# A vision block rewritten per tile of four images: own semaphores and PSUM banks, weights laid out on the host

## The reference

```python
x = x + _L0_conv_ref(_ln_c(x), L0_conv_W_trans)       # q, k, v; softmax over the 3x3 neighbours, 4 heads
t = _to_tokens(x)
t = t + _L0_ffn_ref(_ln_t(t), ...)                    # expert choice: 16 experts take their top 8 tokens of 576
x = _from_tokens(t, x)
x = x + _L1_conv_ref(_ln_c(x), ...)                   # 9x9 patches: y = a @ (b.T @ c) / 9 over 81 patch entries
t = _to_tokens(x)
t = t + _L1_ffn_ref(_ln_t(t), ...)                    # scan of 33 steps; the op is the argmax of token 0
x = _from_tokens(t, x)

def step(h, p):                                       # of _L1_ffn_ref
    op = jnp.argmax(h[0, 0, :NOPS])
    ...                                               # attention, kept only where p['am'][op]
    z = jax.nn.relu(h @ p['w1'][op] + p['b1'][op]) @ p['w2'][op] + p['b2'][op]
    h = jnp.where(p['fm'][op], z, h)
```

## Time and profile before

| what | us |
|---|---|
| median of 3 runs | 162.72 (161.98 to 163.53) |
| span of the profiled execution | 158.8 |
| PE busy | 136.2 (86%) |
| DVE busy | 94.5 (60%) |
| POOL busy | 55.2 (35%) |
| ACT busy | 48.9 (31%) |

### The profile page before, as it was taken

The page is one execution under the profiler, slowest core; times in us unless marked ns, Lnnn a source line. Parts: engine busy times, 40 slices in busy tenths (PEclk is TensorE's granted clock), DMA queues, the critical chain, the costliest instruction groups (busy, mean ns, idle before and its releaser), DMA issues.

```text
span 158.8 us, 2235 instructions
## 1 busy us (share of the span) xinstructions
PE 136.2 (86%) x819; PEld 88.7 (56%) x819; DVE 94.5 (60%) x153; ACT 48.9 (31%) x98; POOL 55.2 (35%) x50
## 2 busy tenths in 40 slices
PE   7959733989999975999899989889999998989960
PEld 4628412655664442666574666663349887567540
DVE  2496699998999999954730122274213122854573
ACT  3460600019000011533734004302262152648540
POOL 8930699000747789999600000000000000027000
PEclk9999995599999999789985555999999999999998
DMA  5525000000000000000000000000000000000003
GB/s 164 136 14 124 15 4 0 0 4 0 2 0 0 0 0 0 0 4 0 0 2 0 0 4 0 0 0 0 0 0 4 0 0 0 0 12 15 0 4 151
DMA packets 7374, 2.62 MB, mean 16 GB/s; under 512 B 5680, under 2 KB 6978, under 8 KB 7363
## 3 DMA queue, kind: packets, MB, share of 16 engines
q1 hardware_dynamic: 7075, 2.04, 5.5%
q10 hardware_dynamic: 288, 0.43, 0.8%
HBM read 1.88 MB, written 0.59 MB: 16 GB/s over the span
## 4 chain that ended last, share of the span: by engine, by line
PE 48%; DVE 40%; ACT 3%; issue 3%; DMA 2%; SPq 1%; DVEq 0%; ACTq 0%
DVE prods L1042 9%; DVE prods L1075 8%; PE PS L709 6%; PE PS L523 6%; PE PS L847 5%; PE PS L493 4%; DVE prods L1093 4%; PE PS L499 4%; PE PS L729 3%; PE PS L742 3%; PE PS L722 3%; DVE rstd L1022 3%; PE PS L700 2%; DMA cst<-consts 2%; PE PS L658 2%
## 5 line engine op out<-in xcount | busy, mean ns | idle before, releaser
L326 POOL TENSOR_TENSOR y<-x,h 128x192 f32<-128x192 f32 x6 | 3.9, 688 | 63.9 <-DVE h L1032 63.9
L493 PE MATMUL PS<-sq 128*128 128x288 f32 x48 | 20.1, 550 | 1.1 <-POOL sq L407 1.1
L876 ACT ACTIVATE sq<-PS 128x288 f32<-128x288 f32 x16 | 6.5, 413 | 41.7 <-PE PS L614 23.7
L1042 DVE TENSOR_TENSOR prods<-q_sb,kpad 128x576 f32<-128x576 f32 x12 | 14.8, 1304 | 2.0 <-ACT kpad L904 2.0
L432 POOL TENSOR_TENSOR prods<-q_sb,kpad 128x576 f32<-128x576 f32 x6 | 10.7, 1822 | 8.2 <-ACT kpad L904 8.2
L577 PE MATMUL PS<-prods,cst 128*32 128x144 f32 x144 | 8.1, 359 | 6.3 <-DVE prods L1042 6.3
L493 PEld LDWEIGHTS PS<-sq 128*128 128x128 f32 x48 | 10.4, 245 | 4.8 <-issue 1.7
L1075 DVE TENSOR_TENSOR prods<-PS,vpad 128x576 f32<-128x576 f32 x18 | 12.5, 745 | 0.0
L523 PE MATMUL PS<-rstd,spread 128*128 128x144 f32 x64 | 8.9, 292 | 3.3 <-DVE rstd L1022 3.3
L523 PEld LDWEIGHTS PS<-rstd,spread 128*128 128x128 f32 x64 | 8.0, 190 | 5.5 <-DVE rstd L1022 5.5
L577 PEld LDWEIGHTS PS<-prods,cst 128*32 128x32 f32 x144 | 4.6, 135 | 9.6 <-DVE prods L1042 8.6
(11 more groups left out here) (165 smaller groups left out, 249.0 us busy)
## 6 DMA issues: line engine op xcount, KB each, us to landing
result<-y SPq DMA_DIRECT2D x2, 288.0 KB, 2.2
prods<-in_x SPq DMA_DIRECT2D x2, 144.0 KB, 3.4
prods<-in_x ACTq DMA_DIRECT2D x1, 288.0 KB, 4.0
ew<-in_L_ffn_weight SPq DMA_DIRECT2D x4, 64.0 KB, 2.5
ew<-in_L_ffn_weight SPq DMA_DIRECT2D x1, 256.0 KB, 3.0
cst<-consts SPq DMA_DIRECT2D x1, 251.0 KB, 3.3
cst<-consts SPq DMA_DIRECT2D x1, 160.0 KB, 3.1
cst<-consts ACTq DMA_DIRECT2D x1, 128.0 KB, 3.4
```

Source lines behind the costliest of these rows:

```text
L493: nc.tensor.matmul(PS[:, bank, 0:HS], sq[:, 0, 0:P], sq[:, 0, 0:HS], start=True, stop=True)
L1042: nc.vector.tensor_tensor(prods[:, t, n, :].rearrange("p (r c) -> p r c", c=WW), q_sb[:, t, :].rearrange("p (r c) -> p r c", c=WW), kpad[: ...
```

## The change

The arithmetic is the same; the kernel around it is written anew.

- **Weights and tables** come laid out from the host in eight arrays (`first`, `pack`, `qkv`, `experts1`, `experts2`, `values`, `masks`, `codes`): block-diagonal weights, selectors, the 65-wide patch matrices. Nothing is turned or built on the chip, and `keep_clock` is gone with all its products.
- **Per tile.** Each tile has its own semaphores and PSUM banks (`AB[t]`, `CD[t]`), and the tiles run shifted: one is in its norm while the other is in its products.
- **Norm.** Ln and Exp with scale -0.5 on ACT give the inverse deviation; the reciprocal on DVE is gone. `widen` uses 64-row selectors.
- **Attention.** q stays in PSUM for DVE's products (POOL reads a copy); v goes by halves through one bank; the softmax's sum is nine products on PE, its inverse Ln and Exp on ACT, and DVE scales the weights before they are spread. `spread` uses four strips of 32 rows, one per quarter of the pixels, each into its own bank; DVE multiplies 24 times (`terms`), POOL adds (`gsum`), PE centres each sum as it comes (`add_centred`).
- **Experts.** `pick` is turned by a product with a diagonal matrix that scales it; hidden has the expert's weights (128 columns) stationary and the four images' tokens moving (16 products a tile); the centring of the next norm is folded into the scatter (`keep_centred`, `scatter`), with a second, uncentred scatter for the residual. ACT changes tables to gelu and back for each tile.
- **conv1.** Groups of 13 channels, laid in runs; one `mab` product of 390 columns with 65 rows per patch row; gram and value of a group come from one product (117 by 181 columns).
- **FFN.** The first layer uses four 32-row strips with one copy of the weights; relu is shared by ACT and DVE; the next op is found from relu and the second weights directly; one operation adds bias and residual. The weights' transfers wait for `step_end`, which DVE gives after the last residual of conv1.

The diff, cut to its core:

```diff
-            def keep_clock(n, bank):
-                for i in range(n):
-                    nc.tensor.matmul(PS[:, bank, 0:HS], sq[:, 0, 0:P], sq[:, 0, 0:HS], start=True, stop=True)
+            def widen(i, t):
+                pe.wait_ge(rstd_rdy[t], i + 1)
+                pe.wait_ge(xc_kept[t], 2 * i + 2)
+                for g in range(2):
+                    for par in range(2):
+                        last = nc.tensor.matmul(PS[:, AB[t][g], par * QS:(par + 1) * QS], sel[64 * g:64 * g + 64, par, :],
+                                                rstd[64 * g:64 * g + 64, t, :], start=True, stop=True)
...
+            def spread(u):
+                t, m = divmod(u, TRI)
+                if t == 0:
+                    pe.wait_ge(attn_rdy, m + 1)
+                for q in range(4):
+                    if u >= 1:
+                        pe.wait_ge(term_rdy, 4 * (u - 1) + q + 1)
+                    nc.tensor.matmul(PS[:, 4 + q, 0:TRI * QS], heads[32 * q:32 * q + 32, t, :],
+                                     attn[32 * q:32 * q + 32, m * TRI:(m + 1) * TRI, :].rearrange("k n s -> k (n s)"),
+                                     start=True, stop=True).then_inc(spread_done, 1)
...
+            def hidden(t):
+                nc.tensor.matmul(PS[:, CD[t][0], 0:ER], con("eb1", E_), con("ebsel", E_), start=True, stop=False, skip_group_check=True)
+                pe.wait_ge(pm_rdy[t], 1)
+                for e in range(E_):
+                    last = nc.tensor.matmul(PS[:, CD[t][0], e * TB:(e + 1) * TB], ew1[:, e, :], pm[:, t, e * TB:(e + 1) * TB],
+                                            start=False, stop=True, skip_group_check=True)
...
+            def expert_out(t):
+                pe.wait_ge(hid_rdy[t], 1)
+                for e in range(E_):
+                    last = nc.tensor.matmul(PS[0:C, CD[t][1], 128 + e * TB:128 + (e + 1) * TB], ew2[:, e, :],
+                                            hidT[:, t, e * TB:(e + 1) * TB], start=False, stop=True, skip_group_check=True)
...
+            def scatter(t):
+                pe.wait_ge(ebd_rdy[t], 1)
+                for g in range(2):
+                    nc.tensor.matmul(PS[:, AB[t][g], 0:HS], flat[:, 1, :], cut(pick, t)[:, g, :], start=False, stop=True,
+                                     skip_group_check=True).then_inc(xc_done[t], 1)
+                pe.wait_ge(ebd_rdy[t], 2)
+                for g in range(2):
+                    nc.tensor.matmul(PS[:, CD[t][g], 0:HS], flat[:, 0, :], cut(pick, t)[:, g, :], start=True,
+                                     stop=True).then_inc(raw_done[t], 1)
...
+            def gsum(t, m):                                     # POOL
+                a = prods[:, t, m * TRI, :]
+                pool.wait_ge(term_rdy, 4 * (TRI * t + m + 1))
+                total = prods[:, 1, 1, :] if (t, m) == (1, 2) else a
+                nc.gpsimd.tensor_tensor(total, a, prods[:, t, m * TRI + 1, :], ALU.add).then_inc(gsum_rdy[t], 1)
+                if m < TRI - 1:
+                    pool.wait_ge(gsum_rdy[t], 2 * m + 1)
+                    nc.gpsimd.tensor_tensor(a, a, prods[:, t, m * TRI + 2, :], ALU.add).then_inc(gsum_rdy[t], 1)
...
+            def product(t, n):                                  # DVE, q in PSUM
+                dy, dx = divmod(n, 3)
+                k = kpad[:, t, dy:dy + HH, dx:dx + WW].rearrange("p (g r) c -> p g r c", g=2)
+                nc.vector.tensor_tensor(prods[:, t, n, :].rearrange("p (g r c) -> p g r c", g=2, c=WW), rows24(both(AB[t])), k,
+                                        ALU.mult).then_inc(prod_rdy[t], 1)
...
+            def inverse_std(i, t):                              # ACT
+                nc.scalar.activation(lnv[:, t, :], PS[:, AB[t][0], 0:QS], ACT.Ln, bias=con(EPS[i])).then_inc(ln_rdy[t], 1)
+                act.wait_ge(ln_rdy[t], i + 1)
+                nc.scalar.activation(rstd[:, t, :], lnv[:, t, :], ACT.Exp, scale=-0.5).then_inc(rstd_rdy[t], 1)
...
+            gram_mask(0, 4)                                     # DVE, conv1
+            residual3(0, 0)
+            choose(0, 0)
+            residual3(0, 1)
+            residual3(0, 2)
+            for k in range(4):
+                gram_mask(1, k)
```

More of the change, by code:

```diff
@@ L24 @@
 V2 = RV * RV
+V2A = V2 + 1
+GRP = 13
+NG = 10
+GW = GRP * NPT
+CP = NG * GRP
 BAND = NP * V2
[L26 to L28 removed]
 NB_, NOPS = 33, 19
[L30 to L41 removed]
@@ new lines, in _ @@
+            pe.wait_ge(gsum_rdy[1], 2)
+            add_centred(1, prods[:, 1, 0, :])
+            widen(1, 0)
+            spread(5)
+            gate(0)
+            pe.wait_ge(gsum_rdy[1], 4)
+            add_centred(1, prods[:, 1, 3, :])
+            for g in range(2):
+                pe.wait_ge(term_rdy, 4 * 5 + 2 * g + 2)
+                for n in (6, 7, 8):
+                    add_centred(1, prods[:, 1, n, :], last=(n == 8), halves=(g,))
+            turn_y(0)
+            variance(1, 1)
@@ new lines, in _ @@
+            turn_pick(0)
+            widen(1, 1)
+            pe.wait_ge(ew1_ld, 16)
+            pe.wait_ge(ew2_ld, 16)
+            pooling(0)
+            keep_centred(0)
+            gate(1)
+            hidden(0)
+            turn_y(1)
+            turn_pick(1)
+            expert_out(0)
+            pooling(1)
+            keep_centred(1)
+            scatter(0)
+            hidden(1)
+            variance(2, 0)
+            expert_out(1)
+            widen(2, 0)
+            scatter(1)
@@ L906, in _, with squares, keep, squares_keep @@
-            for i in range(4):
-                qkv_out(i)
-            for m in range(NBR // TRI):
+            def squares(i, t, g):
+                act.wait_ge(xc_done[t], 2 * i + g + 1)
+                nc.scalar.activation(cut(sq, t)[:, g, :], PS[:, AB[t][g], 0:HS], ACT.Square).then_inc(sq_rdy[t], 1)
+            def keep(t, g):
+                nc.scalar.copy(cut(xc, t)[:, g, :], PS[:, AB[t][g], 0:HS]).then_inc(xc_kept[t], 1)
+            def squares_keep(i, t):
+                for g in range(2):
+                    squares(i, t, g)
+                    keep(t, g)
@@ new lines, in _ @@
+            nc.scalar.preload_act_table_set("natural_log_exp_and_others")
+            act.wait_ge(first_ld, 16)
+            squares(0, 0, 0)
+            squares(0, 0, 1)
+            inverse_std(0, 0)
+            squares(0, 1, 0)
+            squares(0, 1, 1)
+            inverse_std(0, 1)
+            act.wait_ge(kpad_zero, 1)
+            for t in range(T):
+                if t == 1:
+                    act.wait_ge(k_done[1], 2)
+                    nc.scalar.copy(inner(kpad, 1), rows24(both(CD[1]))).then_inc(k_rdy[1], 1)
+                act.wait_ge(q_done[t], 2)
+                nc.scalar.copy(cut(q_sb, t), both(AB[t])).then_inc(q_rdy[t], 1)
@@ new lines, in _ @@
+            keep(0, 0, 0)
+            keep(0, 0, 1)
+            keep(0, 1, 0)
+            keep(0, 1, 1)
+            scale(0, 0)
+            dve.wait_ge(kpad_zero, 1)
+            dve.wait_ge(k_done[0], 2)
+            nc.vector.tensor_copy(inner(kpad, 0), rows24(both(CD[0]))).then_inc(k_rdy[0], 1)
+            scale(0, 1)
+            dve.wait_ge(k_rdy[0], 1)
+            dve.wait_ge(q_rdy[0], 1)
+            for n in range(NDVE):
+                product(0, n)
+            dve.wait_ge(k_rdy[1], 1)
@@ L1052, in _ @@
+            dve.wait_ge(q_rdy[1], 1)
+            for n in range(NDVE):
+                product(1, n)
             dve.wait_ge(score_rdy, 2)
@@ new lines, in _ @@
+            dve.wait_ge(v_rdy, 4)
+            for u in range(5):
+                terms(u)
+            scale(1, 0)
+            terms(5)
+            selection(0)
+            turned_pick(0)
+            scale(1, 1)
+            pooled(0)
+            selection(1)
+            expert_rows(0)
+            turned_pick(1)
+            expert_blocks(0)
+            pooled(1)
+            residual2(0)
+            expert_rows(1)
+            scale_to_patches(0)
+            expert_blocks(1)
+            dve.wait_ge(ones_set, 1)
```

1587 lines of the change are left out of this document (727 added, 860 removed).

## The result

The changed kernel takes 165.19 us (median of 4 runs, 164.27 to 167.39), the kernel before 162.35 on the same chip: ratio 1.0198, 95% interval 1.0107 to 1.0288. It is slower, as forecast, but by 2%, not by 6%.

What follows compares the result with a forecast made beforehand. By stage, DVE paced the spread and PE conv1, with PE busy at half clock in the experts. Start 36, to first pixel product 77, conv1 37, end 18.5, plus 3.9 outside the span, made 172 us; range 152 to 187.

Steps and rivals of the forecast that it cites:

- The base: Time outside the span: median 162.72 less span 158.8 us, taken as 3.9 us and added to every sum.
- The start: Start to the first spread term: 36 us, 4.4 earlier than before, with the first product at 16.
- T0: The time of the first spread term, put at 36 us; later marks are counted from it.
- The spread stage: First spread term to the second tile centred: 22 us, with the four row strips running beside each other.
- the third rival: Row strips don't overlap: +7 us in the spread stage, +2 in the FFN, 181 in all; chance 0.06.
- The experts: Second tile centred to first pixel product: PE at half speed throughout, product 77 us after the first spread term.
- half only from `hidden(0)` on: Routing variant: half speed only from the first hidden layer; first pixel product 71 us after the first spread term.
- conv1: First pixel product to last residual: 37 us, with the clock recovering after some 4 us.
- The end: Last residual to the end, LN3 of one tile and the FFN: 18.5 us, bounds 15 and 23.2.
- the likeliest: Whole kernel, half speed throughout routing and clock recovery in conv1: 165 to 181 us, chance 0.38.
- lost only for routing: Full clock lost only in routing from `hidden(0)` and held elsewhere: 162 us in all, no change; chance 0.10.
- The first rival: The clock holds or comes back: 150 us in all if held throughout; chance 0.28 for faster.

Runs made afterwards that it cites:

- e5: The changed kernel with DVE's twelve attention products reading q from the SBUF copy in place of PSUM: 173.32 us, ratio 1.07 to the kernel before.
- e2: The changed kernel with eleven products of zeros where PE waits in the softmax and first two spreads: 164.47 us, ratio 1.012 to the kernel before.
- e6: The changed kernel with PE's turn of the first token behind the first gram pair of the second tile, not the fourth: 160.25 us.
- e8: The combined kernel: changed kernel plus 64-column `hidden`, fillers (zero products), gelu before Ln and Exp, earlier token, 128-row patch products: 144.35 us, ratio 0.8745 to the kernel before.
- e3: The changed kernel with the second tile's gelu ahead of the first tile's Ln and Exp, two table loads fewer: 161.74 us.

## Why the prediction was right in kind and too large

The profiled execution of the changed kernel took 165.66; the prediction's sum was 172.4. The difference is found term by term; some terms were too long and some too short, so part of the nearness is luck.

- **The base, -2.0.** Median less span gave 3.9 us outside the span. That was the span of one execution against the median of others. Each execution here has 1.8 to 2.2 us outside its own span; 1.9 for this one (165.66 - 163.8). The step "so 3.9 us lie outside it" was wrong.
- **The start, -2.6.** T0 was put at 36 and came at 33.4. The price of a product was right (0.69 taken, 0.67 measured, and e5 shows the cause). The first product was put at 16 by a guess at what a separate tile saves; it came at 13.7, and POOL's six products took 1.29 each (7.72 in all), under the 1.41 that I had as the lower end; e5, where the row gives 1.74 against 1.34, shows that DVE's reading q from PSUM makes the difference.
- **The spread stage, +3.2.** T0 + 22 was put for the second tile centred; it was T0 + 25.2 (to the cut at 58.6, 0.4 before the last product's end). The strips ran beside each other (8 instructions, four strips, 1.01 us), so the third rival fell. What was missing is mostly the clock: 0.56 from 36 to 46. e2 gives 2.2 of it back; the last 1 us is open.
- **The experts, -7.2.** 55 us were put from there to the first pixel product (77 less 22), and it took 47.8. This is the step that failed: "So I take half speed: 77". The mechanism was right, its beginning wrong. PE's work up to the first hidden layer, gates, turns, pooling and centring, ran at a clock of 1.00 for 10 us, busy 10.00 of them, and the fall came in the layer that I had named. The list itself was priced well: those 10.00 us at half speed would be 18.9, and with the 33.20 that PE was busy behind the fall that makes 52.1, where 52.2 had been put. So 8.9 us were put too many by the clock, and 1.6 too few for waits (4.6 against 3). The row that I leaned on, 82 to 86 at 0.52, shows a fall at 82.2, just behind pooling products of 64 moving columns (L658, 2.83 us from 79.10); the products of few moving columns came when the clock was half already. My own variant "half only from `hidden(0)` on" gave T0 + 71 (162 in all); it was T0 + 73, in which the late spread stage lies. I had taken waits in the spread stage as a sign for the routing; the clock came back there by itself at about 45.
- **conv1, -0.6.** 37 was put, 36.4 measured, by another way, so that this term is right by luck: the clock rose 3.3 us behind the first pixel product (4 had been put), then fell a second time at 127, which had no place in the sum. A stall behind `choose` was forecast with 6; PE's gap was 2.2, as e6 shows.
- **The end, +2.5.** 18.5 was put, 21.0 measured. The clock was 0.59 here, but it explains little: in e8 the end took 20.6 at 0.78. From the first product of the FFN's first layer to the first of its second it was 7.4 us here and 6.9 in e8, where 5.5 had been put for the relu pieces; why is open.

-2.0 - 2.6 + 3.2 - 7.2 - 0.6 + 2.5 = -6.7, and 172.4 - 6.7 = 165.7. Of the cases, the truth lies between the likeliest and the middle one, "lost only for routing", which had a chance of 0.10 and 162; in the routing itself it was the middle one. The first rival's price, 150 with the clock held throughout, was about right: with the waits of e3 and e6 gone as well, e8 measures 144.35, its first pixel product at T0 + 57 (59 in the prediction).

## What to carry to other kernels

Read the granted clock beside the busy column: PE can be busy all the time at 0.5. Where its products there have few moving columns, try more, though they be zeros: here 60 columns of zeros cost PE 0.06 us in a layer of 3.73 and DVE 1 us a tile, and the clock held through the layer. Expect little of one such repair alone: the clock can fall again in the next waits; the wide operand gave 1.6 us alone and the fillers lost 0.4, where the combined kernel lost 14.7 without the one and 10.0 without the others. Look at more than one trace before a fall of the clock is put down to an edit: in e3's conv1 it came 3 us later, though the edit touches nothing there. And take the time outside the span from the same execution as the span.
